# Merging equal scatter targets over 512 edges instead of 128, with two partial tables instead of four, in a two-layer graph kernel

## What is computed

```python
feat_neigh = segment_sum(edge_val[:, None] * feat_in[edge_col], edge_row, num_segments=n)
feat_self_trans = _branch(feat_in, W_self, ...)     # relu(x @ W.T + b), normalised
feat_neigh_trans = _branch(feat_neigh, W_neigh, ...)
x = _layernorm(x + feat_self_trans + feat_neigh_trans)
```

## Time and profile before

| | |
|---|---|
| median of the timed runs | 5264.2 us (3 runs, 5263.99 to 5267.14) |
| span of the profiled execution | 6176.2 us |
| instructions | 86140 |
| busy: TensorE, DVE, ACT, POOL | 3676.8, 2879.2, 2789.4, 4072.2 us |
| chain that ended last | TensorE 31%, issue 15% of the span |
| DMA | 587 MB, 95 GB/s over the span |

### The profile page before, as it was taken

How to read it: one execution, slowest core, us unless ns; L and a number is a source line. 1 busy time by engine, 2 the same in 40 slices (tenths; PEclk the granted TensorE clock), 3 DMA queues, 4 the chain that set the end, 5 groups by cost and what they waited for, 6 DMA issues and landing times. The chain is left out here.

```text
span 6176.2 us, 86140 instructions
## 1 busy us (share of the span) xinstructions
PE 3676.8 (60%) x18515; PEld 3020.3 (49%) x18515; DVE 2879.2 (47%) x12091; ACT 2789.4 (45%) x9367; POOL 4072.2 (66%) x3270
## 2 busy tenths in 40 slices
PE   5555555555555555555474667665676666676666
PEld 3333434434333443433254566655565656666655
DVE  6565565556556555655471233333333333333334
ACT  2222222222222222222264567665665766676666
POOL 4888888888888888888745455544554545555552
PEclk7766666666776666667686666677666677766676
DMA  8666666666666666666772222222222222222221
GB/s 275 110 114 114 111 112 116 111 111 115 112 111 112 116 111 111 115 111 108 143 209 66 53 67 63 60 62 56 62 66 58 64 59 64 66 64 59 65 61 43
DMA packets 703023, 587.38 MB, mean 95 GB/s; under 512 B 287194, under 2 KB 572431, under 8 KB 701430
## 3 DMA queue, kind: packets, MB, share of 16 engines
q0 software_dynamic: 285872, 224.40, 26.2%
q1 hardware_dynamic: 394090, 297.48, 17.4%
q10 hardware_dynamic: 23004, 64.87, 2.8%
HBM read 374.12 MB, written 212.29 MB: 95 GB/s over the span
## 5 line engine op out<-in xcount | busy, mean ns | idle before, releaser
L786 POOL DMA_INDIRECT sums_scratch<-vals,to_i x1564 | 2455.1, 1570 | 543.9 <-issue 361.4
L1115 POOL DMA_INDIRECT fg<-f_scratch,src_e x1564 | 1482.7, 948 | 1389.5 <-DMA src_e<-in_src 757.2
L1179 ACT ACTIVATE hot<-raw,e_s 128x40 f32<-128x40 f32 x6272 | 1447.7, 315 | 436.1 <-issue 339.4
L704 PE MATMUL ps_n<-same,hot 128*40 128x128 f32 x3136 | 695.5, 415 | 1317.7 <-issue 1314.7
L704 PEld LDWEIGHTS ps_n<-same,hot 128*40 128x40 f32 x3136 | 556.7, 184 | 1426.8 <-issue 1362.5
L1144 PE MATMUL ps_eu<-hot,prod 128*128 128x120 f32 x3136 | 901.8, 373 | 280.6 <-issue 279.6
L1305 DVE TENSOR_TENSOR prod<-ps_ew,fg 128x256 f32<-128x256 f32 x392 | 164.3, 419 | 1711.0 <-remote 1304.4
L1142 PE MATMUL ps_eu<-hot,prod 128*128 128x40 f32 x3136 | 619.5, 280 | 429.3 <-issue 410.5
L1142 PEld LDWEIGHTS ps_eu<-hot,prod 128*128 128x128 f32 x3136 | 635.6, 242 | 481.0 <-issue 468.8
L1144 PEld LDWEIGHTS ps_eu<-hot,prod 128*128 128x128 f32 x3136 | 627.3, 243 | 299.0 <-issue 298.7
L744 ACT COPY near<-ps_n 40x512 f32<-40x512 f32 x196 | 113.3, 578 | 1420.7 <-PE ps_n L704 931.6
(11 more groups left out here) (210 smaller groups left out, 4269.3 us busy)
## 6 DMA issues: line engine op xcount, KB each, us to landing
srow_s<-in_src SPq DMA_DIRECT2D x194, 512.0 KB
hid_scratch<-hid SPq DMA_DIRECT2D x196, 256.0 KB
hid_e<-hid_scratch SPq DMA_DIRECT2D x196, 256.0 KB
e_s<-in_edge_attr SPq DMA_DIRECT2D x194, 256.0 KB
sums_scratch<-zeros ACTq DMA_DIRECT2D x12, 2112.0 KB, 30.5
sums_scratch<-vals,to_i POOLq DMA_INDIRECT x1564
fg<-f_scratch,src_e POOLq DMA_INDIRECT x1564
t_in<-sums_scratch POOLq DMA_DIRECT2D x72, 256.0 KB, 8.1
```

The costliest lines, as they stand in the source:

```text
L704: last = pe.matmul(ps_n[t // TH][:, t % TH, :], hot[:, k, t, :], same[:, k, t, :], start=True, stop=True)
L786: pool.indirect_dma_start(out=sums_d[i], out_offset=bass.IndirectOffsetOnAxis(ap=to_i[:, j, t:t + 1], axis=0), in_=vals[:, j, t, :], in_of ...
L1115: pool.indirect_dma_start(out=fg[:, j, t, :], out_offset=None, in_=f_d, in_offset=bass.IndirectOffsetOnAxis(ap=src_s[:, j, t:t + 1], axis= ...
L1179: last = act.activation(hot[:, k, t, c, :], raw[:, k, t, :], ACT.Copy, scale=e4_s[:, j, t, c:c + 1])
```

## The change

- The merge runs over the four tiles of a half, 512 edges. Tile i of a half is compared with tiles 0 to i: `same[i]` is 128 x 128(i+1). One scalar_tensor_tensor makes it, with an accumulated sum, where there were a tensor_scalar and a scalar_tensor_tensor. The last 128 columns are masked by `upto` (less or equal), the earlier ones by ones. The sum `upon` is above 1 where an equal edge came earlier, and such an edge goes to a spare row of its own out of 512.
- `ps_n` of a half is made by four products that add into the same bank, of 512, 384, 256 and 128 columns.
- There are two tables, one for each half. The four scatters of a half follow without waits among them; the first waits until the four of that half in the group before have landed. `n_scat` is given ahead of the second half.
- Six zeroing transfers instead of twelve; a table has 102 x 128 rows instead of 99 x 128.
- In the node stage SP loads the blocks of both tables (four blocks ahead instead of eight), and TensorE sums and transposes by two products with the identity; the three accumulating transfers are gone, and POOL's list there is no longer ten blocks behind.

```diff
-NTAB = 4
+NTAB = 2
...
-NPAD = 99 * P
+NPAD = 102 * P
-TR = 8
+TR = 4
...
+                    dve.memset(upto[:, 0:TH - 1, :], 1.0)
...
-                    dve.tensor_scalar(lower[:, :], iota_f[:, :], part_f[:, 0:1], None, ALU.is_lt)
-                    dve.tensor_scalar(spare[:, :], part_f[:, :], float(N), None, ALU.add)
+                    dve.tensor_scalar(upto[:, TH - 1, :], iota_f[:, :], part_f[:, 0:1], None, ALU.is_le)
+                    for i in range(TH):
+                        dve.tensor_scalar(spare[:, :, i], part_f[:, :].to_broadcast([P, 2]), float(N + P * i), None, ALU.add)
...
                             done(dve, n_psn, s, 2)
+                            settle(dve, passed)
+                            done(dve, n_away2, s, 1)
                             for t in range(TS):
-                                last = dve.tensor_scalar(same[:, k, t, :], rows[:, t // TH, t % TH, :], srcf[:, t:t + 1], None,
-                                                         ALU.is_equal)
+                                hf, i = t // TH, t % TH
+                                last = dve.scalar_tensor_tensor(out=same[i][:, k, hf, :, :], in0=rows[:, hf, 0:i + 1, :],
+                                                                scalar=srcf[:, t:t + 1], in1=upto[:, TH - 1 - i:TH, :],
+                                                                op0=ALU.is_equal, op1=ALU.mult,
+                                                                accum_out=upon[:, t:t + 1])
                             last.then_inc(n_same, 1)
...
-                            done(dve, n_before, s, 1)
-                            done(dve, n_away2, s, 1)
-                            for t in range(TS):
-                                last = dve.scalar_tensor_tensor(out=junk[:, t, :], in0=rows[:, t // TH, t % TH, :],
-                                                                scalar=srcf[:, t:t + 1], in1=lower[:, :],
-                                                                op0=ALU.is_equal, op1=ALU.mult,
-                                                                accum_out=before[:, t:t + 1])
-                            last.then_inc(n_before, 1)
-
-                            dve.tensor_scalar(away[:, 0, :], srcf[:, :], -1.0, spare[:, 0:1], ALU.mult, ALU.add).then_inc(n_away, 1)
-                            done(dve, n_before, s)
+                            dve.tensor_tensor(away[:, 0, :], spare[:, :, :].rearrange("p h k -> p (h k)"), srcf[:, :],
+                                              ALU.subtract).then_inc(n_away, 1)
+                            done(dve, n_same, s)
                             done(dve, n_away, s)
-                            dve.scalar_tensor_tensor(out=away[:, 1, :], in0=before[:, :], scalar=1.0, in1=away[:, 0, :],
-                                                     op0=ALU.min, op1=ALU.mult).then_inc(n_away2, 1)
+                            dve.scalar_tensor_tensor(out=away[:, 1, :], in0=upon[:, :], scalar=1.0, in1=away[:, 0, :],
+                                                     op0=ALU.is_gt, op1=ALU.mult).then_inc(n_away2, 1)
...
-                                for t in range(TS):
-                                    last = pe.matmul(ps_n[t // TH][:, t % TH, :], hot[:, k, t, :], same[:, k, t, :],
-                                                     start=True, stop=True)
+                                for hf in range(2):
+                                    for i in reversed(range(TH)):
+                                        last = pe.matmul(ps_n[hf][:, 0:i + 1, :], hot[:, k, hf * TH + i, :],
+                                                         same[i][:, k, hf, :, :], start=(i == TH - 1), stop=(i == 0),
+                                                         skip_group_check=True)
                                 last.then_inc(n_psn, 1)
...
+                            for hf in range(2):
+                                if hf == 0 and isinstance(s, int) and s == NSG - 1:
+                                    continue
+                                if isinstance(s, int) and s == 0:
+                                    pool.wait_ge(z_st[hf], 16 * ZSPLIT)
                                 else:
-                                    pool.wait_ge(added[i], n * 16)
-
-                                settle(pool, n_scat if t == TS - 1 else passed)
-                                pool.indirect_dma_start(
-                                    out=sums_d[i], out_offset=bass.IndirectOffsetOnAxis(ap=to_i[:, j, t:t + 1], axis=0),
-                                    in_=vals[:, j, t, :], in_offset=None, compute_op=ALU.add).then_inc(added[i], 16)
+                                    pool.wait_ge(added[hf], s * TH * 16)
+                                settle(pool, n_scat if hf == 1 else passed)
+                                for t in range(hf * TH, (hf + 1) * TH):
+                                    pool.indirect_dma_start(
+                                        out=sums_d[hf], out_offset=bass.IndirectOffsetOnAxis(ap=to_i[:, j, t:t + 1], axis=0),
+                                        in_=vals[:, j, t, :], in_offset=None, compute_op=ALU.add).then_inc(added[hf], 16)
...
                             done(sp, m_sum, b, TR)
-                            sp.dma_start(flat(t_in[0:used(b), j, :, :]), rows_of(sums_d[0], b)).then_inc(t_ld[j], 16)
+                            for t in range(NTAB):
+                                sp.dma_start(flat(t_in[:, j, t, :, :]), rows_of(sums_d[t], b)).then_inc(t_ld[j], 16)
...
                             for c in range(CB):
-                                last = pe.transpose(ps_n[:, c, :], t_in[:, j, c, :], ident[:, :])
+                                for t in range(NTAB):
+                                    last = pe.matmul(ps_n[:, c, :], t_in[:, j, t, c, :], ident[:, :],
+                                                     start=(t == 0), stop=(t == NTAB - 1))
```

More of the change, by code:

```diff
@@ L127, in graph_layers @@
         base_i = sb("base_i", [1, NH], I32)
-        lower = sb("lower", [P, P])
-        spare = sb("spare", [P, 1])
+        upto = sb("upto", [P, TH, P])
+        spare = sb("spare", [P, 2, TH])
         npass_i = sb("npass_i", [1, 1], I32)
@@ L413, in graph_layers @@
             hot = tmp("hot0", [P, 2, TS, W])
-            same = tmp("same", [P, 2, TS, P])
-            junk = tmp("junk", [P, TS, P])
-            before = tmp("before", [P, TS])
+            same = [tmp(f"same{t}", [P, 2, 2, t + 1, P]) for t in range(TH)]
+            upon = tmp("upon", [P, TS])
             away = tmp("away", [P, 2, TS])
@@ L446, in graph_layers @@
             added = [sem(f"n_added{i}") for i in range(NTAB)]
-            n_srcf, n_rel, n_hot, n_same, n_before = sem("n_srcf"), sem("n_rel"), sem("n_hot"), sem("n_same"), sem("n_before")
+            n_srcf, n_rel, n_hot, n_same = sem("n_srcf"), sem("n_rel"), sem("n_hot"), sem("n_same")
             n_away, n_away2, n_to, n_psn, n_near = sem("n_away"), sem("n_away2"), sem("n_to"), sem("n_psn"), sem("n_near")
@@ L468, in loads_so_far @@
                 return q if j < NPRE else q + 1
-            assert IDLE % NTAB == 0 and IDLE % 2 == 0
+            assert IDLE == TH
             npass = nc.values_load(npass_i[0:1, 0:1], min_val=1, max_val=N // W + 1)
@@ L767, in _ @@
                     def _(pool):
-                        def adds_so_far(i, s, t):
-                            return (s - 1) * PER + t // NTAB + len(range(i, TS, HEAD) if i < HEAD else ())
                         def body(s, q, j):
@@ L789, in _ @@
                         sweep(pool, body, 0, NSG, 4, 192)
-                        for i in range(NTAB):
-                            pool.wait_ge(added[i], 16 * (adds_so_far(i, NSG, 0) - IDLE // NTAB))
+                        pool.wait_ge(added[0], 16 * TH * (NSG - 1))
+                        pool.wait_ge(added[1], 16 * TH * NSG)
                         pool.dma_reset(range(min(x.num for x in added), max(x.num for x in added) + 1))
@@ L822, in graph_layers @@
             b_in = tmp("b_in", [NP, UN, CB, D])
-            t_in = tmp("t_in", [NP, TR, CB, D])
+            t_in = tmp("t_in", [NP, TR, NTAB, CB, D])
             blank = tmp("blank", [P, 2 * NT // NB])
@@ L844, in graph_layers @@
             t_ld = [sem(f"m_t_ld{i}") for i in range(TR)]
-            t_acc = [sem(f"m_t_acc{i}") for i in range(TR)]
             m_sum, m_blank = sem("m_sum"), sem("m_blank")
@@ L871, in body @@
                             sp.dma_start(flat(b_in[0:used(m), i, :, :]), rows_of(base_d, m)).then_inc(b_ld[i], 16)
-                    sweep(sp, body, 0, NB + 7, 16, 24, TR)
+                    sweep(sp, body, 0, NB + 3, 8, 24, TR)
                 @block.gpsimd
@@ L878, in body @@
                     def body(b, q, j):
-                        for t in range(1, NTAB):
-                            m, r, i = at(b, q, j, 2 * t - 1, TR)
-                            if live(m):
-                                if t == 1:
```

(10 more changed lines are left out.)

16 lines of the change are left out of this document (3 added, 13 removed).

## The result

The changed kernel takes 5796.1 us (median of 4 runs, 5793.2 to 5798.4), the kernel before 5265.7 beside it: a ratio of 1.101, 95% interval 1.099 to 1.102. The prediction was 5612 us, slower, range 5280 to 5885. Some runs of a kernel fall in a slower state, over 1.5% above its fastest; ratios leave these out, so a ratio can differ by a few thousandths from the quotient of two medians. The profiled execution of the changed kernel has a span of 5791.4 us, so here profile and timed runs agree, which for the kernel before they did not.

The account below looks back on a forecast made before the run. GpSimd's issue bounds the scatter stage at 14.97 us a group; after the change a circle of waits through VectorE, TensorE and ScalarE does, at 17.0. 5264 + 375 (scatter stage) - 27 (node stage) = 5612 us, range 5280 to 5885.

Parts of the forecast that it names:

- second circle: Scatter stage: waits from VectorE through TensorE and ScalarE back to `hid`, 11.3 us a group, growing to 17.0 against GpSimd's 14.97.
- The eight wide comparisons: VectorE, ahead of `ps_n`: eight wide operations take 4.49 us for 1.98, 2.5 more; bounds 0.9 less and 0.6 more.
- `ps_n`: TensorE, scatter stage: 2560 columns for 1024, beginning at the low clock, take 6.7 us, 3.2 more; range 6.2 to 7.5.
- The circle: Scatter stage, one turn of the waits: 9.9 us before, plus 2.5 for the comparisons and 3.2 for `ps_n`.
- The self branch and the table load: Scatter stage, added to each turn: 1.1 us on average for self result and statistics, 0.3 for reloading the sigmoid's table.
- The pace and the end of the stage: Scatter stage: 17.0 us a group, first scatter at 56, end at 3382 against 3007, +375 us.
- Node stage: After the scatters: start 16.5 us less, 24 blocks 10 less, together -27 us, from -34 to +12.
- the 24 us: Start of the node stage before the change, to its first transpose: read as four landings in a row, 6 us each.
- Gather stage: Last stage: bound by its issue in timed runs and unchanged; the profile's extra 912 us were placed here.
- A: Rival, scatter stage: GpSimd (POOL) keeps the bound, turn of waits 14.4 us, time 5216 us; chance 5%.
- B: Rival, TensorE: high clock throughout, comparisons as taken, turn of waits 15.3 us, time 5280 us; chance 5%.
- C: Rival, TensorE: low clock through `ps_n` and `ps_h`, turn of waits 20.0 us, time 6197 us; chance 5%.

Follow-up runs that it names:

- the kernel with the later `hid`: Changed kernel with `hid` of group s-1 made in group s, behind the eight `hot`: 6139.9 us against 6140.5 of the kernel before, ratio 0.997.
- the repeated run of the later `hid`: Changed kernel with `hid` made one group later, measured again where the gather stage is short: 5289.9 us against 5259.5 of the kernel before, ratio 1.0058.

## Why the prediction was right, and where it was off

The mechanism was right: a second circle, hidden at 11.3 us, comes out from under GpSimd's 14.97 and sets the pace. Opening it by one move gave back 501 of the scatter stage's 545 us, and the same move did nothing in the kernel before. The time of 5612 came out 184 us too low. The sizes, by the prediction's steps:

- *The eight wide comparisons.* Taken 4.49 us, measured 5.64. This is the term that was mis-sized. The nearest form gave the first 128 columns well (0.363), since it read with the same stride, but the 1.03 ns for each column more came from two-input operations that read neighbours; these read every fourth word, at 1.77. The bound above, 0.6 more, was put on the first 128 columns and missed the true value. In front of them comes a step that no term held: 0.48 us from the CAST to the first comparison (1530.77 to 1531.25), where the kernel before had 0.20 (1536.95 to 1537.15). Over the changed kernel VectorE stands idle 32.3 us before the comparisons, 18.6 of it until `srcf` is there; both kernels wait for `srcf`, and why it shows now was not tried.
- *`ps_n`.* Taken 6.7 us, measured 6.22 on average; the range 6.2 to 7.5 just held it. It began at 0.50 as said and rose after some 3 us, not 4.0, and at the high clock the whole takes 4.50, not 5.0.
- *The circle.* 9.9 + 2.5 + 3.2 = 15.6 without the self branch, measured 16.5: 1.15 for the comparisons and 0.28 for the step before them more, 0.5 for `ps_n` less. That the two errors have opposite signs, so that a third of the first is hidden, is luck. The self branch and the table load were taken as 1.4 a group, and 17.9 - 16.5 = 1.4.
- *The pace and the end of the stage.* 17.0 against 17.9: 0.9 x 195 = 176 us. The first scatter came at 47.9 and not 56: earlier than before the change. Eight of those 176 us come back so. The prediction named six zeroing transfers fewer and costed them at nothing; whether they are why it comes early was not tried.
- *Node stage.* Taken -27, measured -37.8. The start gained 20.8 in place of 16.5, since the first product of the node stage came 3.4 us into it, not 7 to 8:

```profile
3555.19 3.79 PE L892 MATMUL ps_mn<-ident,t_in 128*128 128x128 f32 x16 [14.72 <-DMA t_in<-sums_scratch]
```

So the reading of the 24 us as four landings of 6 each was wrong: two plain loads with the barrier take 3.4, and the three accumulating transfers took most of the 24. The Trainium skill, DMA: Bandwidth & Descriptors, Anatomy of one DMA, gives its 2.6 us (an estimate from its figures) for a transfer issued by GpSimd; that lies nearer to these 3.4 than the 6 did, but it prices the three accumulating ones far too low, so its total gain (8 less) is further off than that of the rows. The blocks took 6.7 us on average, the low bound, not 7.0: from GpSimd's first `y_m` at 3572.32 to its last at 3734.01 are 161.7 us for 24 blocks, against 177.6. The kernel before had blocks of 6.7 too (3218.79 to 3225.48); its mean of 7.4 came from blocks of up to 9.3 us, of which the changed kernel has one (9.4). So the gain in the blocks is mostly that the long ones are gone, and not a shorter usual block.
- *Gather stage.* Taken as unchanged; it lost some 25 us, at least 16 of them by the longer gathers. That the 912 us by which the profile of the kernel before exceeded its timed runs lay in the gather stage is borne out: the kernel with the later `hid` has a profile with a long gather stage and one with a short, and its first gather stands at 3261 in a span of 6191 us and at 3257 in one of 5295.
- *Rivals.* A (GpSimd keeps the bound) and B (high clock throughout) both needed TensorE at 1.00 from the start of `ps_n`; the clock was at 0.50 in the group shown. A needed the comparisons at their lower bound besides. With unused products to keep it up the circle was 16.5 and not B's 15.3, since the comparisons were under-sized there too. C didn't occur: `ps_eh` took 1.12 us. The Trainium skill's page TensorE: Matmul & The Clock Gate, Part 1, has the clock follow how busy TensorE recently was; the runs agree in kind (4.50 us behind busy TensorE, 6.05 after 10.6 us of idleness), but the idle part of the circle was enough to keep the clock low where `ps_n` began, against A.

The sum of it: 5612 + 176 - 8 - 11 + 25 = 5794, against 5796 measured.

## What to carry to other kernels

When one engine bounds a loop, walk the other closed circles of waits before you lengthen anything on them: add up one turn, compare it with the bound, and the difference is all you may spend; here it was 3.7 us and the change spent 6.6. Look for a way to open a circle before you shorten it: here the last operation of a group, moved behind the first ones of the next, added no work and gave back 501 us, where the faster comparison gave 292 and the higher clock 275. And take the price of an operation from a row with the same access pattern, not only the same form and width.

## What the runs showed of the hardware that was not expected

- A `scalar_tensor_tensor` that reads every fourth word of an int32 row: 1.77 ns a column and 0.44 us for 128 columns, against 1.04 and 0.35 for neighbours, and these the same for int32 and float32. Other strides, and float32 with a stride, were not tried.
- Some scatters are stretched while VectorE runs long operations. The median is 1545 to 1548 ns in all kernels. In the repeated run of the later `hid`, of 200 scatters that lay beside a comparison of 512 strided columns for over 0.8 us, 68 took more than 1.8 us; of 791 with no comparison beside them, 5 did. An example from the first run of that kernel:

```profile
1025.59 1.15 DVE L644 SCALAR_TENSOR_TENSOR same<-srow_s,srcf,upto 128x512 f32<-128x512 int32 x1
1025.73 2.38 POOL L785 DMA_INDIRECT sums_scratch<-vals,to_i  x1 [0.30 <-issue]
```

The mean was 1607 to 1611 ns with strided comparisons, 1568 with contiguous ones and 1560 with narrow ones, all three bound by GpSimd. With shorter comparisons most of the stretch goes; through what the two engines meet was not tried.

- TensorE's clock can fall in a short pause: after 2.38 us of idleness behind 5.4 us of products at 1.00 the next 3 us were granted 0.65.
- The same program's gather stage takes 2.0 ms in some comparisons and 2.9 in others, with GpSimd waiting for loads of 4 KB (`src_e`: 22.5 us in the short profile of the later `hid`, 721.5 in the long one). The same kernel did both, so the program alone doesn't decide it; what does was not found.
